# The first 16 edge columns get their slots ahead of the other 141, and the block one-hots become one operation

## The reference

```python
x = _layernorm(x + _L0_gnn_ref(x, stack([src, dst], 1), W, b, a))          # attention over edges
x = _layernorm(x + _L1_gnn_ref(x, edge_attr_4, edge_attr_32, stack([src, dst]), ...))
# L0: emb = x @ W + b;  e = exp(leaky_relu(s[src] + t[dst]))
#     results = segment_sum(e * emb[dst], src) / segment_sum(e, src)
# L1: per edge, w = ssp(edge_attr @ W_f1) @ W_f2 * (ssp(s0 @ W_s1) @ W_s2);
#     messages from x[edge_src] and edge_sh, summed with segment_sum over edge_dst; then linear layers
```

## Time and profile before

| | us |
|---|---|
| median of 3 runs (lowest to highest) | 1200.53 (1197.57 to 1201.22) |
| the profiled execution, its own time | 1203.19 |
| its span in the profile | 1201.5 |
| PE busy in the span | 928.1 (77%) |
| DVE | 837.1 (70%) |
| POOL | 746.7 (62%) |
| ACT | 517.3 (43%) |

### The profile page before, as it was taken

How to read it: one execution, slowest core, us unless ns; L and a number is a source line. 1 busy time by engine, 2 the same in 40 slices (tenths; PEclk the granted TensorE clock), 3 DMA queues, 4 the chain that set the end, 5 groups by cost and what they waited for, 6 DMA issues and landing times. The chain is left out here.

```text
span 1201.5 us, 22376 instructions
## 1 busy us (share of the span) xinstructions
PE 928.1 (77%) x5255; PEld 617.3 (51%) x5256; DVE 837.1 (70%) x2120; ACT 517.3 (43%) x1489; POOL 746.7 (62%) x774
## 2 busy tenths in 40 slices
PE   1316645369999986872999999999999999999664
PEld 1204322135555543762666666666666666666443
DVE  8451010057777775771899999999999999999537
ACT  1203211023232331561566666666666666666311
POOL 2777777577777770122667777777777776777212
PEclk9997766789999997885899999999999999999768
DMA  9300101178888882024555555555555555554002
GB/s 345 76 14 25 33 25 40 40 214 239 240 240 238 241 223 37 31 88 135 171 174 175 167 176 164 182 159 177 165 179 167 173 172 172 174 171 148 31 0 88
DMA packets 107464, 171.51 MB, mean 143 GB/s; under 512 B 36038, under 2 KB 79162, under 8 KB 107292
## 3 DMA queue, kind: packets, MB, share of 16 engines
q0 software_dynamic: 31584, 122.92, 32.9%
q1 hardware_dynamic: 72060, 46.71, 12.8%
q10 hardware_dynamic: 3776, 1.38, 0.5%
HBM read 151.61 MB, written 19.35 MB: 142 GB/s over the span
## 5 line engine op out<-in xcount | busy, mean ns | idle before, releaser
L750 PE MATMUL ps<-ring,aw 128*128 128x512 f32 x332 | 187.8, 654 | 22.9 <-DVE aw L698 16.2
L1085 POOL DMA_INDIRECT ring<-tab_d,ed x166 | 160.6, 967 | 62.0 <-issue 32.3
L409 POOL DMA_INDIRECT slots_d<-stage,stage_pos x157 | 153.3, 977 | 71.3 <-issue 49.0
L1095 POOL TENSOR_TENSOR dot<-ring,ed 128x768 f32<-128x768 f32 x83 | 122.2, 1472 | 119.1 <-issue 91.0
L1126 PE MATMUL ps<-mm_sb,oh 128*128 128x512 f32 x332 | 183.5, 635 | 15.9 <-DVE acc L1268 15.9
L667 POOL DMA_INDIRECT ring<-xt_d,ed x166 | 159.1, 958 | 58.5 <-issue 45.7
L1128 PEld LDWEIGHTS ps<-mm_sb,ohs 128*128 128x128 f32 x996 | 141.1, 196 | 82.2 <-issue 82.2
L1188 ACT ACTIVATE ohs<-oh,ed 128x128 f32<-128x128 f32 x498 | 161.6, 389 | 0.0
L1219 ACT ACTIVATE S_sb<-ps 128x512 f32<-128x512 f32 x166 | 90.1, 595 | 129.4 <-PE ps L1175 129.4
L1128 PE MATMUL ps<-mm_sb,ohs 128*128 128x128 f32 x996 | 141.7, 280 | 0.0
L1242 DVE TENSOR_TENSOR ps<-S_sb,ps 128x1024 f32<-128x1024 f32 x83 | 102.0, 1229 | 20.7 <-ACT S_sb L1219 20.0
(11 more groups left out here) (213 smaller groups left out, 1850.8 us busy)
## 6 DMA issues: line engine op xcount, KB each, us to landing
ilb<-f_d SPq DMA_DIRECT2D x83, 128.0 KB
ed<-slots_d SPq DMA_DIRECT2D x166, 38.0 KB, 3.4
tab_d<-tabrow SPq DMA_DIRECT2D x5, 896.0 KB, 3.7
f_d<-ft SPq DMA_DIRECT2D x83, 38.0 KB
slots_d<-fill SPq DMA_DIRECT2D x7, 418.0 KB, 4.5
ring<-xt_d,ed POOLq DMA_INDIRECT x166, 4.1
hcat<-f_d SPq DMA_DIRECT2D x83, 32.0 KB
s0b<-f_d SPq DMA_DIRECT2D x83, 32.0 KB
```

Source lines behind the costliest of these rows:

```text
L409: g.indirect_dma_start(slots_d[:, :], bass.IndirectOffsetOnAxis(ap=stage_pos[:, h, k:k + 1], axis=0), stage[:, h, k, :], None).then_inc(sc ...
L750: pe.matmul(ps[:, 2 * u, :], aw[:, r, k, :], xg[:, c, k, 0:D], start=(alone or k == 0), stop=(alone or k == 1))
L1085: gp.indirect_dma_start(xj[:, r, k, :], None, tab_d[:, :], bass.IndirectOffsetOnAxis(ap=ed[:, c, k, JD:JD + 1].bitcast(I32), axis=0))\
L1095: gp.tensor_tensor(dot[:, u, :, :, :], xj[:, r, :, P:D].rearrange("p k (m n) -> p k m n", m=3), ed[:, c, :, IL + 2:IL + 5].unsqueeze(3).to ...
```

## The change

Four things, all in the first block:

1. The ten one-hot planes are made by one `tensor_tensor` on 1570 columns (`blk` and `iota` by broadcast), which needs `iota` (`pool_c` 6).
2. After the ten-column operations, `first_places` works out the slots of columns 0 to 15 alone, with operations on all ten planes at once (160 columns). `other_places` works out columns 16 to 156 in the old way, at the start of `rows(1)`, that is after batch 0 has been staged.
3. DVE, ACT and PE wait for 12 counts of `pool_c` and not 14, so no more for the clearing of `acc`. POOL's own program is unchanged.
4. On PE the two `rowtot` matmuls stand behind `hidden_f(0)`, and not ahead of it.

```diff
-                for q in range(NB):
-                    ins = v.tensor_scalar(oh10[:, q, :], blk[:, :], float(q), None, ALU.is_equal)
-                link(v, ins)
-                v.wait_ge(pool_c, 14)
+                v.wait_ge(pool_c, 6)
+                link(v, v.tensor_tensor(oh10[:, :, :], blk[:, :].unsqueeze(1).to_broadcast([EP, NB, EC]),
+                                        iota[0:EP, 0:NB].unsqueeze(2).to_broadcast([EP, NB, EC]), ALU.is_equal))
+                v.wait_ge(pool_c, 12)
...
+                def places(cols):
+                    link(v, v.tensor_tensor(inc[:, :, cols], inc[:, :, cols], oh10[:, :, cols], ALU.mult))
+                    link(v, v.tensor_reduce(slot[:, cols], inc[:, :, cols].rearrange("p b c -> p c b"), AX.X, ALU.add))
+                    link(v, v.tensor_copy(slot_i[:, cols], slot[:, cols]))
+                    v.tensor_scalar(slot_t[:, cols], slot_i[:, cols], 7, None, ALU.arith_shift_right)
+                    link(v, v.tensor_scalar(slot_p[:, cols], slot_i[:, cols], P - 1, None, ALU.bitwise_and))
+                    link(v, v.scalar_tensor_tensor(rowpos[:, cols], slot_p[:, cols], float(NT), slot_t[:, cols], ALU.mult, ALU.add))
+                def first_places():
+                    cols, size = slice(0, NS), [EP, NB, NS]
+                    link(v, v.tensor_tensor(past[:, :, cols], inc[:, :, cols], paired[:, :].unsqueeze(2).to_broadcast(size), ALU.is_ge))
+                    v.tensor_tensor(inc[:, :, cols], inc[:, :, cols], off[:, :].unsqueeze(2).to_broadcast(size), ALU.add)
+                    link(v, v.tensor_tensor(past[:, :, cols], past[:, :, cols], jump[:, :].unsqueeze(2).to_broadcast(size), ALU.mult))
+                    link(v, v.tensor_tensor(inc[:, :, cols], inc[:, :, cols], past[:, :, cols], ALU.add))
+                    places(cols)
+                def other_places():
+                    cols = slice(NS, EC)
+                    for q in range(NB):
+                        ins = v.tensor_scalar(past[:, q, cols], inc[:, q, cols], paired[:, q:q + 1], jump[:, q:q + 1], ALU.is_ge, ALU.mult)
+                    link(v, ins)
+                    for q in range(NB):
+                        ins = v.scalar_tensor_tensor(inc[:, q, cols], inc[:, q, cols], off[:, q:q + 1], past[:, q, cols], ALU.add, ALU.add)
+                    link(v, ins)
+                    places(cols)
+                first_places()
                 def rows(b, h):
                     cols = bass.ds(b * NS, NS)
+                    if isinstance(b, int) and b == 1:
+                        other_places()
...
-                        act.wait_ge(pool_c, 14)
+                        act.wait_ge(pool_c, 12)
...
-                pe.wait_ge(pool_c, 14)
-                pe.wait_ge(rowtot_ready, 1)
-                pe.matmul(ps[:, 3, 0:NB], ones[0:EP, :], rowtot[:, :], start=True, stop=True)
-                pe.matmul(ps[0:EP, 4, 0:NB], below[0:EP, 0:EP], rowtot[:, :], start=True, stop=True).then_inc(base_ready, 1)
-
+                pe.wait_ge(pool_c, 12)
...
+                    if isinstance(b, int) and b == 0:
+                        pe.wait_ge(rowtot_ready, 1)
+                        pe.matmul(ps[:, 3, 0:NB], ones[0:EP, :], rowtot[:, :], start=True, stop=True)
+                        pe.matmul(ps[0:EP, 4, 0:NB], below[0:EP, 0:EP], rowtot[:, :], start=True, stop=True).then_inc(base_ready, 1)
```

## The result

The changed kernel takes 1189.1 us (median of 5 runs, 1181.15 to 1192.46), the kernel before 1198.23 us (median of 5, 1197.57 to 1201.22): a measured ratio of 0.9903, 95% interval 0.9878 to 0.9929, which is 11.6 us.

The account below looks back on a forecast made before the run. The prediction took POOL's start and scatter speed to bound the first block. Starting 13.0 us earlier, less 1.0 us of contention, gives 12.0 us off 1200.53: 1188.5 us, with 1185 to 1194.5 to hold 8 in 10.

Parts of the forecast that it names:

- What bounds the block: First block: POOL's start and its scatters' speed set the end; from the first scatter on it only scatters, 202.3 us.
- One-hots not held up: DVE's new one-hot operation runs beside POOL's clearing, takes 1.79 us and ends at 5.65, 4.4 us earlier.
- the rival: POOL's clearing holds up the new one-hot operation too: slots 8.8 us earlier, time 1192.5; chance 0.17.
- PE's order: On PE, rowtot matmuls behind hidden_f(0) start at 10.5 and not 9.85: the new order costs 0.65 us.
- Slots of 16 columns: DVE's slots for batch 0 take 2.7 us against 12.0, bounds 2.3 to 3.3.
- First scatter: POOL's first scatter starts at 18.35 instead of 31.35, 13.0 us earlier.
- Given back: POOL's scatters beside DVE's two-input work on the other columns take longer: 0.6 to 2.0 us lost, taken as 1.0.
- Batches 1 and 2: Both staged before POOL asks: batch 1 at 29.5 against 38.7, batch 2 at 54.7 against 60.7.
- The rival on the slower side: Late ACT weight loads make batch 2 too late for POOL: slower than before, say 1204.5 us; chance 0.02.
- The crawl: Scatters from 18.35 to 31 us slow down under full DMA load: time 1191 to 1196; chance 0.12.
- The blocks behind: Blocks behind the first start from the barrier and simply shift; otherwise the prediction is wrong.
- Sum: First block: 13.0 - 1.0 = 12.0 us gained, off 1200.53, giving a median of 1188.5.

Follow-up runs that it names:

- e1: The kernel before with only the one-operation one-hots and the wait for 12 constants instead of 14: ratio 0.9972 to the kernel before.
- e3: The changed kernel with POOL clearing acc by copying a tile of zeros, so that the clearing reads SBUF: ratio 0.9912 to the kernel before.
- the repeat: The changed kernel as it is, run again on the same chip as three other kernels: ratio 0.9901 to the kernel before.
- e9_best2: The changed kernel with scores reading from PSUM and the rowtot matmuls between transposes and matmuls of hidden_f(0): ratio 0.9874 to the kernel before.
- e4: The changed kernel with the two rowtot matmuls and their wait ahead of hidden_f(0), as before: one run, 1190.31 us.
- e6: The changed kernel with scores reading the broadcast vector from PSUM, not ACT's copy in SBUF: ratio 0.9896 to the kernel before.
- e5: The changed kernel with the mask of the other 141 columns applied five times instead of once: ratio 0.9937 to the kernel before.
- e7: The changed kernel with scores from PSUM, rowtot matmuls between transposes and matmuls of hidden_f(0), and loc_i behind the row totals: ratio 0.9885 to the kernel before.
- e2: The changed kernel with the ten one-hot operations of before, so the split of the slots alone: ratio 0.9942 to the kernel before.

## Why the prediction was right

- *What bounds the block.* Right, and the experiments carry it: over eleven profiles with first scatters from 17.49 to 31.35 us, the next block starts 206.7 to 210.4 us after the first scatter, and what is left when the scatters' busy time is taken off is 54.3 to 54.4 us in all eleven. So every difference in that stretch is scatters that took longer.
- *One-hots not held up.* Taken 1.79 us, end 5.65; measured 1.79 and 5.53. e1 puts their worth, with the wait for 12 constants, at 4.66 us (working: 4.4). This was the step that was chosen between two bounds 4.9 us apart; e3 shows that the choice hung on what POOL's operation does: it writes only. With a reading one the forecast would have missed by 4.2 us. By the rival, the time would have been 1192.5 and the first scatter near 22.5. The trace agrees with the rule of the Trainium skill, "SBUF — State Buffer", section "Who interferes with whom", in both halves: 1.79 us beside a writing operation, 7.57 instead of 3.43 beside a reading one.
- *PE's order.* The sum had DVE going on at 11.55; it was 11.15, since the edge rows landed 3.9 instead of 4.3 us after their issue. In the repeat, at 4.3 us, it was 11.51. The step was called a cost of 0.65 us. Against a PE that is free it costs something (e9_best2 gains 0.43 at the first scatter, though its edge rows landed 0.8 us later). Against the old order it does not cost 0.65: there `hidden_f(0)` is the later one, which the prediction did not weigh, and the first scatter of e4, 18.25, lies within those of the changed order, 17.92 to 18.62. This part of the change is worth nothing that the runs can tell.
- *Slots of 16 columns.* 2.7 us taken, 2.87 measured; the reduction of 160 columns takes 0.44 and not 0.36.
- *First scatter.* 18.35 taken, 17.92 and 18.29 measured; the difference of the two is the landing of the edge rows.
- *Given back.* 1.0 us taken, 1.0 measured (154.3 against 153.3 us), but that the two agree so well is in part luck. The prediction had three or four scatters at 0.2 us each, or one that waits for a whole mask (1.6), and gave as a sign a few scatters of 1.16 us or more between 20 and 25 us. There is one, of 1.63, which gives 0.67 of the 1.0; the rest is the first scatter (1.34 us, before 1.21; DVE ran L299 beside it, which has one tensor input, and the cause is open) and four that took 0.03 to 0.08 us more. e6 shows for 512 columns that it is DVE's second SBUF input, and e5 that the scatters slow down as long as the masks run. The Trainium skill, "SBUF — State Buffer", section "Who interferes with whom", infers that a `tensor_tensor` does not stall descriptor generation; that was weighed in the prediction and does not hold here: 1.36 against 0.96 us beside the masks of e5. (The 1.16 us that the prediction set against it stand beside a `scalar_tensor_tensor`.)
- *Batches 1 and 2.* Batch 1 staged at 29.2 (taken: 29.5). Batch 2 was taken for 54.7 and staged at 53.1, with POOL asking at 60.30. Two things came out otherwise. ACT's weight loads took 18.7 us and not 15.4 in the full DMA load and ended at 39.08 instead of 36.3, which cost nothing, since ACT waited for PE until 46.22. And PE's part of batch 2 ran in about half the time (L519 in 1.16 us, before 2.07). That belongs to this one execution: in the repeat L519 took 2.07 us again and batch 2 was staged at 54.8. The rows of the first profile:

```profile
35.22 3.86 ACTq L468 DMA_DIRECT2D w<-W_f  x8
46.22 1.02 ACT L487 ACTIVATE wa_bc<-ps 128x1024 f32<-128x1024 f32 x1 [25.11 <-PE ps L530]
...
49.16 1.16 PE L519 MATMUL ps<-x 128*128 128x128 f32 x8 [0.69 <-ACT x L456]
52.41 0.69 DVE L326 SCALAR_TENSOR_TENSOR stage<-ps,x 128x512 f32<-128x512 f32 x1 [9.47 <-ACT x L463]
```

  The rival on the slower side needed loads 14 us late to be felt; they were 3.
- *The crawl.* The scatters of 18 to 31 us took 0.96 us but for the first and for some beside DVE's two-input work (1.03, 1.04, 1.63 and 0.99). The full DMA load did not slow POOL, though it lasts longer now, since the weight loads fall into it (before, the share was 0.31 in these 6 us):

```profile
30.00:36.00 6.00, 0.00 (x0) 0.00 (x0) 5.37 (x21) 0.00 (x0) 4.47 (x6) 1.00 1.11 337
```
- *The blocks behind.* That they don't simply shift was named as a sign of being wrong, and in the first profile they were 9.7 us shorter. The repeat was 2.7 us shorter there and no other profile more than 3.6, so the 9.7 us stay with that one execution.
- *Sum.* 12.0 us forecast, 12.4 and 12.0 in the block's end, 11.6 (8.5 to 14.6) by the ratio. That the median came within 0.6 us of 1188.5 is partly luck: the forecast started from 1200.53, and the kernel before had a median of 1198.23 beside it.

## What to carry to other kernels

When one engine works through a long list without a pause, look for what its first item waits for: work out the first batch alone, as far as the shape of the data allows, and lay the rest behind it, under the list. Beside a POOL that issues indirect DMAs, give DVE's operations at most one input in SBUF where PSUM holds the other anyway. Moving a short DVE operation by 0.3 us can cost more than it is worth when it changes which of DVE and POOL comes first.

## What the runs showed of the hardware that was not expected

- A scatter beside back-to-back two-input operations of 512 columns takes 1.16 us, beside those of 1410 columns 1.35, against 0.96. A single mask of 1410 columns held one scatter for 1.63 or 1.64 us in six profiles and two scatters for 1.35 each in e3 and e7, where the scatters lay otherwise to it. In all of these the scatter ends about 0.8 us after a DVE operation starts (e5: mask at 23.44, scatter until 24.24; changed: L282 at 24.34, scatter until 25.13; L367 at 63.19, scatter until 63.98). That fits a scatter held until the running operation ends, so that the price depends on where in the operation it comes; no run tries this by itself.
- Some one-input operations of DVE end only with POOL's clearing, though it only writes: a copy of 9 columns took 0.64 instead of 0.17 us (e7_best, ending 0.03 us behind the clearing), and the first one-hot 4.92 (before and e2, 0.1 us behind it). That the clearing is what held them is read from these ends; no run moves it away from the old one-hots. That a two-input operation gets through beside the same clearing makes the one with more reads the better choice there.
- The running sum (`tensor_tensor_scan`) counts as a two-input operation in this: 7.57 instead of 3.43 us (e3_readclear).
- The last block, on the same instructions, took 67.4 to 73.7 us in the ten profiles read for it, at granted clocks of 0.70 to 0.80; the three longest, 73.5 to 73.7 us, are at 0.70, the shortest at 0.77. What decides the clock was not tried. The differences are as large as the smaller effects here, so these were read in the first block's rows and not in the time.
